# Key tiles of the cross-attention in rounds of two, with four score banks and a ring of three

## The reference

```python
x = x + xattn(layernorm(x), ctx, ctx, Wq, bq, Wk, bk, Wv, bv, Wo, bo)   # ctx: 8 x 1601 x 256, 16 heads of 16
x = x + attn(layernorm(x), in_proj_weight, out_proj_weight)             # causal self-attention, 16 heads
x = x + ffn(layernorm(x), Wg, bg, W1, b1, W2, b2)                       # 8 experts of 1024, the best 2 by softmax
```

## Time and profile before

| | |
|---|---|
| median of 3 runs | 676.38 us |
| profiled execution | 677.73 us, span 675.9 us |
| TensorE busy | 648.0 us (96%), 6410 instructions |
| VectorE busy | 472.3 us (70%) |
| ScalarE, GpSimd busy | 326.6 us (48%), 298.5 us (44%) |
| mean granted clock | 0.992 of 2.4 GHz |
| chain that ended last | TensorE 78%, VectorE 9%, issue 5%, GpSimd 5% |

### The profile page before, as it was taken

One profiled execution on the slowest core, in us unless ns is written; L12 is line 12 of the kernel. 1 busy time (PEld: TensorE's weight loads), 2 busy tenths in 40 slices (PEclk: granted clock), 3 DMA queues, 4 the chain that ended last, 5 costly groups with the idle time before them and its releaser, 6 DMA issues.

```text
span 675.9 us, 15772 instructions
## 1 busy us (share of the span) xinstructions
PE 648.0 (96%) x6410; PEld 532.6 (79%) x6418; DVE 472.3 (70%) x870; ACT 326.6 (48%) x533; POOL 298.5 (44%) x386
## 2 busy tenths in 40 slices
PE   7989999999999989999998999888999999999996
PEld 4778878778868867877886886656789999999996
DVE  4887757676759787585877865668777567667653
ACT  4355655654554554554455544355544444444421
POOL 1137797996766788596668758200000000000000
PEclk9999999999999999999999999989999999999999
DMA  5411110100010010010000000053003302330000
GB/s 164 147 47 53 31 46 26 50 26 25 27 50 2 26 50 25 27 50 26 27 25 26 1 2 1 22 230 126 1 1 126 124 10 118 124 124 0 0 0 32
DMA packets 12852, 34.11 MB, mean 50 GB/s; under 512 B 1515, under 2 KB 9972, under 8 KB 10612
## 3 DMA queue, kind: packets, MB, share of 16 engines
q1 hardware_dynamic: 12756, 33.19, 14.8%
q0 software_dynamic: 32, 0.01, 0.0%
HBM read 32.67 MB, written 0.52 MB: 49 GB/s over the span
## 4 chain that ended last, share of the span: by engine, by line
PE 78%; DVE 9%; issue 5%; POOL 5%; ACT 2%; DMA 0%; POOLq 0%; DVEq 0%; ACTq 0%
PE bank L1154 44%; PE bank L1163 9%; PE bank L1345 9%; POOL prob_sum L481 5%; PE bank L1331 4%; PE bank L1224 3%; PE bank L1264 2%; PE bank L1273 2%; DVE prob_sum L481 1%; DVE maxes L877 1%; DVE ctx_lo L465 1%; ACT k_hi L615 1%; PE bank L1248 1%; DVE k_lo L858 1%; PE bank L1375 1%
## 5 line engine op out<-in xcount | busy, mean ns | idle before, releaser
L481 POOL TENSOR_TENSOR prob_sum<-probs,prob_sum 128x256 f32<-128x256 f32 x336 | 268.5, 830 | 73.6 <-ACT probs L719 68.2
L719 ACT ACTIVATE probs<-bank 128x1024 f32<-128x1024 f32 (+1 forms) x104 | 106.7, 1026 | 115.3 <-PE bank L1345 102.2
L877 DVE TENSOR_REDUCE maxes<-bank 128x1 f32<-128x400 f32 (+1 forms) x256 | 129.4, 564 | 22.7 <-PE bank L1224 22.3
L701 ACT ACTIVATE h_raw<-bank,b_sb 128x512 f32<-128x512 f32 (+2 forms) x72 | 46.2, 642 | 106.7 <-PE bank L1154 106.6
L1154 PE MATMUL bank<-w_hi,h_hi 128*128 128x256 f32 x256 | 72.6, 284 | 0.0
L1154 PE MATMUL bank<-w_hi,h_lo 128*128 128x256 f32 x256 | 72.1, 282 | 0.0
L1154 PE MATMUL bank<-w_lo,h_hi 128*128 128x256 f32 x256 | 72.0, 281 | 0.0
L858 DVE SCALAR_TENSOR_TENSOR k_lo<-bank,bias_sb,k_hi 128x400 fp32r<-128x400 f32 (+2 forms) x64 | 40.4, 631 | 44.6 <-ACT k_hi L615 44.6
L1163 PE MATMUL bank<-probs,v_sb 128*32 128x128 f32 (+1 forms) x1664 | 68.3, 283 | 2.5 <-DVE masked L812 2.0
L1345 PE MATMUL bank<-qbd_hi,k_hi 64*128 64x256 f32 (+1 forms) x416 | 67.8, 321 | 0.0
L1154 PE MATMUL bank<-wv_hi,ctx_hi 128*128 128x256 f32 (+1 forms) x208 | 65.1, 313 | 2.7 <-DVE maxes L877 2.4
(11 more groups left out here) (157 smaller groups left out, 1420.9 us busy)
## 6 DMA issues: line engine op xcount, KB each, us to landing
raw<-in_w SPq DMA_DIRECT2D x16, 1024.0 KB, 6.8
ctx_raw<-in_ctx_t SPq DMA_DIRECT2D x16, 400.0 KB, 3.6
ctx_raw<-in_ctx_t SPq DMA_DIRECT2D x8, 402.0 KB, 3.8
ctx_raw<-in_ctx_t SPq DMA_DIRECT2D x8, 399.0 KB, 3.5
w_sb<-in_w_t SPq DMA_DIRECT2D x1, 1280.0 KB
w_raw<-in_w_t SPq DMA_DIRECT2D x2, 256.0 KB, 4.8
result<-x_all SPq DMA_DIRECT2D x1, 512.0 KB, 3.0
x_all<-in_x SPq DMA_DIRECT2D x1, 384.0 KB, 4.4
```

The costliest lines, as they stand in the source:

```text
L481: ins = engine.tensor_tensor(prob_sum[0:ROWS[k], cols], probs[0:ROWS[k], s % 2, cols], acc[0:ROWS[k]], ALU.add)
L701: nc.scalar.activation(h_raw[:, c % 2, 0:width], bank[:, at, 0:width], ACT.Gelu, bias=b1_sb[:, bass.ds(e, 1), c:c + 1].rearrange("p a b -> ...
L719: nc.scalar.activation(probs[0:ROWS[k], s % 2, :].rearrange("p (g n) -> p g n", g=G), bank[0:ROWS[k], score_bank(b, k):score_bank(b, k) + ...
L877: nc.vector.tensor_reduce(maxes[:, g * PAIRS + j, c:c + 1], src[:, 0:width], AX.X, ALU.max).then_inc(read_dve, 1)
```

## The change

Key tiles 0 to 11 of a batch are worked in pairs, key tile 12 alone; batch 7 (the second of the last tile) stays with single key tiles. A round does, on TensorE, shift product, first pair of maxima, scores and further maxima of the one key tile, the same of the other, then the key, chain and value units of both, and then both weighings. For this,

- the scores alternate between banks 0-1 and 2-3 in all batches, and the units' ring is left with banks 4 to 6: unit n waits for unit n-3;
- there are three probability buffers instead of two, and two sums of probabilities instead of one;
- the maxima of a round stand in its front, on VectorE too, ahead of all other units of the round; `M_AT` puts them at key tiles 2 to 11 (so 6, 6, 6, 8 and 6 units per round), `find_shift` follows those of round 10-11, and `X` comes after the scores of key tile 12 instead of ahead of them;
- on ScalarE both exponentials come first and then the units, on GpSimd a reciprocal root stands ahead of the round's last sum;
- the prologue keeps five banks; in the last tile the chain is up to one key tile later from `st10` on; the rest of the queries (`p1` to `r3`) are made at key tiles 4 to 9 of batch 0.

The diff, cut to its core:

```diff
-RING_BANKS = range(2, 7)
-LATE_BANKS = range(4, 7)
+RING_BANKS = range(4, 7)
+PROLOGUE_BANKS = range(2, 7)
+PROB_BUFFERS = 3
-V_AT = {3: [0, 1]} | {k: [k - 2] for k in range(4, KT)}
+V_AT = {k: [k - 2] for k in range(2, KT)}
+def rounds(paired=True):
+    width = 2 if paired else 1
+    return [list(range(k, min(k + width, KT))) for k in range(0, KT, width)]
-M_AT = in_order({1: 2, 2: 2, 3: 2, 4: 1, 5: 2, 6: 2, 7: 1, 8: 2, 9: 2})
+M_AT = in_order({2: 1, 3: 2, 4: 1, 5: 2, 6: 1, 7: 2, 8: 2, 9: 2, 10: 1, 11: 2})
-REST_CHAIN = {3: ["p1"], 5: ["r1"], 6: ["p2"], 8: ["r2"], 9: ["p3"], 11: ["r3"]}
+REST_CHAIN = {4: ["p1"], 5: ["r1"], 6: ["p2"], 7: ["r2"], 8: ["p3"], 9: ["r3"]}
-FIND_SHIFT_AT = KT - 3
+FIND_SHIFT_AT = KT - 2
...
         def score_bank(b, k):
-            return ROW_TILES * (k % 2) if isinstance(b, int) and b == B - 1 else 0
+            return ROW_TILES * ((b * KT + k) % 2)
...
+            def exponential(b, k):
+                n = b * KT + k
+                act.wait_ge(scores_done, n + 1)
+                if n >= PROB_BUFFERS:
+                    act.wait_ge(pv_done, n - PROB_BUFFERS + 1)
+                    act.wait_ge(summed, n - PROB_BUFFERS + 1)
...
# VectorE
             def tile(t, units, more, chain):
+                for steps in units.rounds:
...
+                    if chain and paired:
+                        chain_between(units, steps[0], t - 1)
+                    if first_k == 0 and more > first_bi:
+                        next_batch_queries(2 * t + first_bi, first_bi)
+                    for s in steps:
+                        for m, kind, u in units.front[s]:
+                            unit(units, m, kind, u, t - 1, 2 * t + first_bi + 1, (first_bi + 1) % 2)
+                    if FIND_SHIFT_AT in [divmod(s, KT)[1] for s in steps] and more > first_bi:
...
                         find_shift()
+                    for s in steps:
...
+                        for m, kind, u in units.at[s]:
+                            unit(units, m, kind, u, t - 1, b + 1, (bi + 1) % 2)
...
# TensorE
             def shift_scores(units, b, bi, k):
...
+                if n >= 2:
                     pe.wait_ge(exp_done, n - 1)
...
+                for steps in units.rounds:
+                    bi, first_k = divmod(steps[0], KT)
+                    b = 2 * t + bi
+                    last_batch = b == B - 1
+                    if last_batch and first_k == 2:
+                        weigh(b, 0)
+                    for s in steps:
+                        k = s % KT
                         shift_scores(units, b, bi, k)
+                        for n, kind, u in units.front[s][:ROW_TILES]:
+                            unit(units, n, kind, u, t - 1, b + 1, (bi + 1) % 2)
+                        scores(b, bi, k)
+                        for n, kind, u in units.front[s][ROW_TILES:]:
+                            unit(units, n, kind, u, t - 1, b + 1, (bi + 1) % 2)
+                    for s in steps:
+                        if s % KT == 1 and not is_first(b):
+                            denominators(b - 1)
+                        for n, kind, u in units.at[s]:
+                            unit(units, n, kind, u, t - 1, b + 1, (bi + 1) % 2)
+                    for s in steps:
+                        k = s % KT
+                        if not last_batch:
+                            weigh(b, k)
+                        elif k >= 2:
+                            weigh(b, k - 1)
```

More of the change, by code:

```diff
@@ L655, in step @@
                 for n, kind, u in units.at[s]:
-                    if not (kind == "X" and units is not PROLOGUE):
-                        unit(units, n, kind, u, t, b, parity)
+                    unit(units, n, kind, u, t, b, parity)
             def prepare(k):
@@ L733, in _ @@
+            for t in range(TT - 1):
+                tile(t, TILES[t], 2)
             tile(TT - 1, LAST, 1)
@@ new lines, in tile @@
+            def tile(t, units, more, chain):
+                for steps in units.rounds:
+                    first_bi, first_k = divmod(steps[0], KT)
+                    paired = len(steps) > 1
+                    if chain and paired:
[6 more added lines that the diff above has]
+                    if FIND_SHIFT_AT in [divmod(s, KT)[1] for s in steps] and more > first_bi:
+                        n = max(n for s in steps for n, kind, _ in units.front[s])
@@ L1066, in _ @@
             tile(0, FIRST, 2, False)
             for t in range(1, TT - 1):
[L1068 removed]
+                tile(t, TILES[t], 2, True)
             tile(TT - 1, LAST, 1, True)
@@ L1425, in _ @@
+            for t in range(TT - 1):
+                tile(t, TILES[t])
             tile(TT - 1, LAST)
-            weigh(B - 1, 1, KT - 1)
+            weigh(B - 1, KT - 1)
             denominators(B - 1)
```

289 lines of the change are left out of this document (116 added, 173 removed).

## The result

The changed kernel takes 690.94 us (median of 4 runs, 688.26 to 691.67), beside 676.99 us for the kernel before in the same session (4 runs, 676.06 to 678.49): 1.0193 times as long, with a 95% interval of 1.0171 to 1.0215. Forecast were 688.4 us. The profiled execution took 691.67 us with a span of 689.5.

What follows compares the result with a forecast made beforehand. TensorE was taken to bound the attention stage, with VectorE answering for most of its banks. Pairing's savings against waits for three banks summed over the batches to +12.0 us on 676.4, so 688.4 us, range 683 to 692 (chance 0.45).

Steps and rivals of the forecast that it cites:

- What a pair saves: Paired key tiles in seven batches: each pair loses one change of each kind, 0.39 us, 16.4 us over 42 pairs.
- The banks: Rounds' maxima: three banks instead of five make TensorE wait for VectorE; 2.1 us a batch alone, 35 us walked over seven batches.
- Round 10-11 of second batches: Maxima wait on VectorE behind the routing, 4.29 us, and a split, 0.98; M3 starts at 4.3 instead of 1.2: 3.1 lost.
- second sum: Second batches, key unit's residual to shift's end: VectorE's 14.55 us plus 3.0 for six more maxima make 17.6.
- Batch 4: First batch of a tile: 56.9 us less 2.34 and 0.1, plus 5.0 of waits, so +2.6 us.
- Batches 0 and 1: No such chain between them; 3.5 us lost against 2.3 and about 1 to 2 of own waits: +0.5 us each.
- Batches 6 and 7: Last tile: first batch 3.2 us lost against 3.6, so 0; second +1, self-attention outputs standing ahead of the heads.
- rival c: Waits in round 10-11 of second batches halve the clock, 1.7 us each: 692 to 698; chance 0.22 with other ways above forecast.
- The wait for the shift: TensorE's 1.83 us wait for the shift rows goes: 1.7 us for each of batches 3 and 5, 0.4 for the rest.
- (a): Rounds 4-5 and 10-11: VectorE keeps up and the gain shows, 660 to 675 us; chance 0.23 below 675.
- (b): Whole kernel: the change does what it says but both sides cancel, 675.5 to 677.5 us; within the 0.10 for 675 to 683.
- (d): Round's end: the weighing waits for the second exponential, 1.33 plus 1.03 us after the shift product; given nothing.

## Why the prediction was right, and where not

- **What a pair saves.** Right: 0.39 us forecast, 0.41 to 0.45 measured on five pairs without waits. For all 42 pairs, 16.4 us, it is worked out and not measured: in the other rounds it can't be told from the waits.
- **The banks.** Right in kind and in sum. Batches 0 to 6 came out 9.2 us longer, 11.4 at the same work; with 42 x 0.39 that is 27.8 us lost beyond the waits removed. The forecast had 11.0 + 16.4 = 27.4. Batches 2 to 5 last 58.1 to 59.7 us, as forecast. The waits stand where they were put: from the fourth maxima product of a round on, most of all in rounds 8-9 and 10-11, with VectorE's reductions as releaser, 20.9 us of the weight loads' time.
- **Round 10-11 of second batches.** Oversized: 3.1 us forecast, 1.70 in the trace (1.58 of them lost). The term that was mis-sized is the routing's 4.29 us, taken over from the earlier trace rows. In the changed kernel it took 3.2 (244.11 to 247.32); and it began 0.3 us earlier in the round. So the first maxima were taken up 2.24 us after the shift product at 245.98, not 3.7. The prediction's second sum, 17.6 us from the residual to the shift's end, is 16.7 in the trace (236.42 to 253.16). Rounds 8-9 had gaps of 1.35 and 0.48 us (at 240.10 and 241.06) beside the 2.0 forecast.
- **Batch 4.** Oversized by 1.4 us. Round 8-9 of batch 4 has gaps of 1.12 and 0.48 us (295.52 and 296.49) where 2.5 were forecast. What made up the rest wasn't separated.
- **Batches 0 and 1.** The prediction's own terms, 3.5 us lost against 2.3 and 1 to 2 of waits gone, make -0.8 to +0.2, not the +0.5 that it adds up. Batch 1 came out at -0.2. Batch 0 was undersized, +3.7. Its round 2-3 loses 1.29 us before a maxima product (47.89) for the residual of a key unit, and round 4-5 1.23 us for maxima (58.06); the residuals, which hold the same banks, were not in the walk.
- **Batches 6 and 7.** Forecast 0 and +1, measured -1.7 and +5.0. The prediction says that both self-attention outputs now stand in batch 7, but moves no time for them: 2.24 us went over. At the same work it is +0.5 and +2.8. Of the 2.8, 2.0 are idle time: 1.19 for the normalised rows, 0.53 more for the gates, 0.25 more for the heads, and this last is all there is of the wait that the +1 stood for. That leaves 0.8 for the clock (at most 1.7) and all else. I had looked for the clock (rival c) at the 3.1 us in batches 3 and 5; these waited 1.2 us without a product and kept 1.00. It fell where it fell before, in batch 7, and for 6.8 us more. The rival's mechanism was real, its place and its size were not.
- **The rest.** Forecast 0, measured +0.9. It goes with the 3.4 us at the lower level at 478.3: the two kernels with the earlier chain have none behind batch 7, and their rest is 214.7 us.
- **The wait for the shift** is gone, as forecast. From before alone its removal is worth about 0.9 us in each of batches 3 and 5, not 1.7; in sum 2 us of 676 (0.9977). That the two batches came out only 0.6 and 0.7 us under the forecast is luck in part: this term and that of round 10-11 were both too large, with opposite sign.
- **Rivals.** (a), that VectorE keeps up, falls on the waits; even with reductions a third as long the changed kernel is only as fast at like clocks as the kernel before with the same. (b), the balance, falls by 1.9%. (d), a weighing that waits for its exponential, doesn't show in batches 0 to 6.

So the total of +12.0 came out at +14.0 between medians, or +10 to +13 at like clocks, with errors of opposite sign: batches 3 to 5 forecast too long by 2.7 us and batch 1 by 0.7, batch 0 too short by 3.2 and batches 6 and 7 together by 2.3. The mechanism was right; that the sum is so near is luck in part.

## What to carry to other kernels

Regrouping work on the busiest engine to save its own changeovers paid here what a timeline of one quiet stretch says, 0.4 us a pair; what it costs is read from the other side, from the list of the engine that frees the buffers: take each burst against the length of the ring, and ask what stands ahead of its first reader. An engine at 68% that returns buffers in order can hold up one at 94%. And when a few microseconds decide, split every difference into waits, clock and work that has crossed the line at which you cut, before you explain it, and compare runs at like clocks.
